# Softmax attention with 48 and 49 contraction rows and 17 value columns in place of 63, 64 and 32

## What is computed

```python
x = x + _layernorm(_L0_attn_ref(_layernorm(x, axis=-1), L0_attn_w_attn, L0_attn_w_proj), axis=-1)
x = x + _layernorm(_L0_ffn_ref(_layernorm(x, axis=-1), ...), axis=-1)
x = x + _layernorm(_L1_attn_ref(_layernorm(x, axis=-1), ...), axis=-1)   # linear attention
x = x + _layernorm(_L1_ffn_ref(_layernorm(x, axis=-1), ...), axis=-1)
```

```python
attn = jnp.einsum('bhqd,bhkd->bhqk', q, k) * scale
attn = jnp.where(causal[None, None], attn, -jnp.inf)
sm = jax.nn.softmax(attn, axis=-1)
out = jnp.einsum('bhqk,bhkd->bhqd', sm, v)
```

## Time and profile before

| | |
|---|---|
| median of 3 runs | 4012.15 us (4011.11 to 4018.99) |
| profiled execution, its time | 4022.0 us |
| its span (first to last instruction) | 4020.2 us |
| PE busy | 3221.1 us, 80% |
| PEld busy | 2353.4 us, 59% |
| DVE busy | 2413.5 us, 60% |
| ACT busy | 1504.5 us, 37% |
| mean granted TensorE clock | 0.884 of full speed |

### The profile page before, as it was taken

One profiled execution on the slowest core, in us unless ns is written; L12 is line 12 of the kernel. 1 busy time (PEld: TensorE's weight loads), 2 busy tenths in 40 slices (PEclk: granted clock), 3 DMA queues, 4 the chain that ended last, 5 costly groups with the idle time before them and its releaser, 6 DMA issues. The chain is left out here.

```text
span 4020.2 us, 61755 instructions
## 1 busy us (share of the span) xinstructions
PE 3221.1 (80%) x20641; PEld 2353.4 (59%) x20641; DVE 2413.5 (60%) x6322; ACT 1504.5 (37%) x2158; POOL 809.5 (20%) x873
## 2 busy tenths in 40 slices
PE   6859888888887666596655768998666499999998
PEld 5633333333333565495434556776565488888887
DVE  5557777777774677661227865544677444444444
ACT  2316666666666333242005650000233233333333
POOL 0011111121112222245765651000122000000000
PEclk9868999999999788698658988999777699999999
DMA  7893455444551565644658996665444513233332
GB/s 191 240 157 51 75 85 79 72 71 75 84 77 36 170 216 176 236 141 118 139 116 262 345 309 190 217 200 160 142 156 147 171 45 84 83 83 83 83 83 52
DMA packets 448954, 553.07 MB, mean 138 GB/s; under 512 B 96592, under 2 KB 301424, under 8 KB 447600
## 3 DMA queue, kind: packets, MB, share of 16 engines
q1 hardware_dynamic: 436992, 527.15, 49.3%
q0 software_dynamic: 10240, 14.16, 2.1%
q10 hardware_dynamic: 1648, 10.81, 0.8%
HBM read 312.85 MB, written 238.61 MB: 137 GB/s over the span
## 5 line engine op out<-in xcount | busy, mean ns | idle before, releaser
L545 ACT ACTIVATE att_pr<-att_e_ps 128x1024 f32<-128x1024 f32 (+2 forms) x640 | 596.2, 940 | 326.8 <-PE att_e_ps L597 323.2
L573 PE MATMUL att_m_ps<-att_ks,att_qs 63*128 63x512 f32 (+3 forms) x1536 | 493.9, 446 | 125.1 <-DVE att_mx L510 54.1
L573 PEld LDWEIGHTS att_m_ps<-att_ks,att_qs 63*128 63x128 f32 x1536 | 233.3, 191 | 520.6 <-DVE att_mx L507 185.8
L507 DVE CUSTOM_DVE_ANT_0 att_kept<-att_m_ps,att_causal 128x128 f32<-128x128 f32 (+3 forms) x1024 | 448.3, 487 | 76.1 <-PE att_m_ps L573 52.2
L510 DVE TENSOR_REDUCE att_mx<-att_m_ps 128x1 f32<-128x512 f32 x512 | 329.6, 686 | 158.4 <-PE att_m_ps L573 154.8
L614 PE MATMUL att_o_ps<-att_pr,att_vs 128*32 128x512 f32 (+3 forms) x3072 | 338.2, 513 | 28.3 <-issue 28.1
L486 POOL TENSOR_SCALAR_AFFINE_SELECT att_pr<-att_pr 128x256 f32<-128x256 f32 (+1 forms) x384 | 186.5, 486 | 850.7 <-PEq L588 814.2
L597 PE MATMUL att_e_ps<-att_qs,att_ks 64*128 64x512 f32 (+3 forms) x1536 | 321.1, 376 | 1.8 <-ACT att_pr L545 1.3
L2138 DVE TENSOR_TENSOR ffn_hid<-ffn_gate,ffn_u_ps 128x512 f32<-128x512 f32 x192 | 132.1, 688 | 251.4 <-PE ffn_u_ps L720 208.1
L2186 ACT ACTIVATE ffn_hh<-ffn_hid 128x512 fp32r<-128x512 f32 x192 | 121.6, 633 | 422.8 <-DVE ffn_hid L2142 320.7
L2148 DVE TENSOR_TENSOR ffn_hl<-ffn_hid,ffn_hh 128x512 fp32r<-128x512 f32 x192 | 133.0, 693 | 141.9 <-ACT ffn_hh L2186 141.9
(11 more groups left out here) (287 smaller groups left out, 8075.3 us busy)
## 6 DMA issues: line engine op xcount, KB each, us to landing
prj_o<-attended SPq DMA_DIRECT2D x32, 1024.0 KB
ffn_wt<-weights SPq DMA_DIRECT2D x16, 2048.0 KB
att_qs<-q_high SPq DMA_DIRECT2D x128, 128.0 KB, 5.5
att_ks<-k_high SPq DMA_DIRECT2D x128, 128.0 KB, 7.0
attended<-att_ot SPq DMA_DIRECT2D x64, 256.0 KB, 2.0
prj_x<-x SPq DMA_DIRECT2D x32, 512.0 KB, 5.9
x_high<-prj_xh SPq DMA_DIRECT2D x32, 512.0 KB, 2.8
x_low<-prj_xl SPq DMA_DIRECT2D x32, 512.0 KB, 3.8
```

The lines of the kernel that those rows point to most:

```text
L507: e.tensor_tensor_reduce(kept[:, n % MBUF, 0:w], m_ps[:, n % MBUF, 0:w], causal[:, BLK - w:], 1.0, -3e38, ALU.add, ALU.max, mx[:, h, at, q ...
L545: e.activation(out, src, ACT.Exp).then_inc(exp_done, 1)
L573: e.matmul(m_ps[:, (2 * i + n) % MBUF, 0:w], qs[rows, j, p, q * P:(q + 1) * P], ks[rows, j, p, h * BLK:h * BLK + w], start=True, stop=True ...
```

## The change

Three numbers and what hangs on them. The maximum pass contracts over the 48 rows that hold data, where it took 63; the row for the maximum is row 48 of each half instead of row 63, so the scores contract over 49 rows, where they took 64; and a product with the values loads 17 columns for each head, where it loaded 32. The zero columns behind the last head, and the memset that wrote them, go. Nothing is added, and no instruction changes its place: on every engine the rest stands in the same order with the same semaphores, except that PE's first wait counts two constants instead of three. Partitions 17 to 31 of each head's strip of `o_ps` are no longer written by PE; they keep the zeros of the memset of `o_ps` (L497), and are copied and stored as before. The two halves (64 rows) and the four strips (32 partitions) on which the matmuls are placed in the array remain.

```diff
-    HALF, MAXROW, VSTEP = P // 2, P // 2 - 1, GH * VW + 32 - VW
+    HALF, MAXROW, VSTEP = P // 2, 3 * HD, GH * VW
...
-                e.memset(vs[:, :, :, GH * VW:].rearrange("p j k c -> p (j k) c"), 0.0).then_inc(consts_pe, 1)
                 e.memset(o_ps[:], 0.0).then_inc(consts_pe, 1)
...
                     for hd in range(GH):
-                        i = e.matmul(o_ps[32 * hd:32 * hd + 32, BLK - w:BLK], vs[:, j, k, hd * VW:hd * VW + 32],
+                        i = e.matmul(o_ps[32 * hd:32 * hd + VW, BLK - w:BLK], vs[:, j, k, hd * VW:(hd + 1) * VW],
                                      pr[:, u % NPR, hd // 2, hd % 2, 0:w], start=k == 0, stop=k == 4 * h + 3)
...
-                e.wait_ge(consts_pe, 3)
+                e.wait_ge(consts_pe, 2)
```

## The result

The changed kernel takes 4210.95 us (median, 4206.82 to 4214.52), the kernel before 4015.57 in the same comparison: ratio 1.0486, 95% interval 1.0467 to 1.0504, +195 us. Forecast was 4400 in a range of 4150 to 4570. The direction and the cause were right, and 4211 lies in the range, near its lower end; the likeliest value had twice the growth that came.

A forecast was written before the change was run, and what follows sets the result against it. PE was taken to bound the attention once slow: 31 groups x 13 us at 1.2 GHz = 403, less 23 already paid, plus 9 for the last group, +389; forecast 4400 us, range 4150 to 4570.

The forecast's parts named there:

- PE is thus the bound as soon as it is slow.: Softmax attention: PE is fullest, busy 78.84 of 90 us; 6.8 us at 1.2 GHz cost a group 2.61 us.
- Busy time alone doesn't tell when the clock is full.: First maximum passes: PE busy 29.53 of 40 us at clock 0.50; wide work, products above all, stands where full clock holds.
- the rival of no change: Attention clock stays, as the chip counts halves and strips or busy time: 4012 less at most 5 us; chance 0.12.
- No row shows whether the chip counts the rows and columns that an instruction names or the halves and strips on which it is placed.: Attention matmuls: left open; costs 0 if nothing is counted differently, otherwise the clock is lost.
- the weight 17/32 = 0.53: Products with the values: with 17 columns for 32 they fill 0.53 of the array they filled before.
- Stretch (c): Attention, 450.6 to 454.39 us: no products run, clock then falls with PE 82% busy; taken to show little to spare.
- Once at 1.2 GHz nothing in the loop is as wide as what brought the clock back. I take it that the whole phase then runs at 1.2 GHz.: Whole attention phase at 1.2 GHz: +389 us, forecast 4400; chance 0.72.
- The rival of partial low clock: Attention clock falls but products bring it back repeatedly; about half the phase at 1.2 GHz: +195, 4207 us; chance 0.13.
- The price at 1.2 GHz: Attention group at 1.2 GHz: products +7.7, scores +3.4, maxima +4.9 us, less PE's idle waits; taken as +13 us.
- the upper end of +17.9: Attention group at 1.2 GHz costs at most +17.9 us, from a whole stretch taking 1.58 times as long; gives 4553 us.
- The rival "faster": Idle time before product matmuls, 28.3 us, shrinks with shorter weight loads: 3984 us at the most; chance 0.03.
- Cost of the memset and of the DMAs at nothing: Before the loop: removed memset gains 0 to 0.5 us; the row maximum takes the same two DMAs.

The follow-up runs named there:

- e3: Kernel before with only the maximum pass cut from 63 to 48 rows (scores 64 rows, products 32 columns): 4117.80 us, ratio 1.0252.
- e7: Kernel before with 56 rows in the maximum pass and 57 in the scores, 32 value columns: 4109.85 us, ratio 1.0222.
- e11: Kernel before with only the scores cut to 49 rows (maximum pass 63 rows, 32 value columns): 4104.11 us, ratio 1.0203.
- e2: Kernel before with only the products cut from 32 to 17 columns (63 and 64 rows kept, memset kept): 3999.15 us, ratio 0.9954.
- e9: e2 with the transposition of the maxima issued twice in each group, once for nothing: 4010.11 us, ratio 0.9977 of the kernel before.
- e4: Kernel before, shapes kept, with the product matmuls of the unit of step 16 issued ahead of the maximum matmuls: 4009.42 us, ratio 0.9982.
- e8: Changed kernel plus 8 extra matmuls a group (128 rows, 128 columns, 512 elements), results overwritten: 4182.33 us, ratio 1.0407 of the kernel before.
- e10: e5 plus two extra matmuls a group of 128 rows and 512 elements, ahead of score steps 3 and 9: 4000.43 us, ratio 0.9952 of the kernel before.
- e12: Changed kernel with the transposition of the maxima issued twice in each group: 4239.83 us, ratio 1.0560 of the kernel before.
- e5: Kernel before with 17 value columns, 63 and 64 rows, and the products of the unit of step 16 issued first: 4012.90 us, ratio 0.9983.
- e1: Kernel before with only the rows cut (maximum pass 48, scores 49), products keeping 32 columns: 4250.26 us, ratio 1.0571.

## Why the prediction was right in direction and cause, and wrong in size

- **"PE is thus the bound as soon as it is slow."** Right. All 190.5 us lie between the merges; the busy time of DVE, ACT and POOL stayed.
- **"Busy time alone doesn't tell when the clock is full."** Right, and e3 shows it best: groups busy for 27.16 us as before, then 23 us at half clock, with no instruction more or less. The Trainium skill ("TensorE: Matmul & The Clock Gate", Part 1: The HAM clock gate) has the gate watch how busy PE is; by that the rival of no change should have come, at 4012. The trace goes against it in this form: with groups at full clock that are busy for one and the same 88%, maximum passes of 48, 56 and 63 rows give clocks of 0.87 (e3), 0.86 (e7, scores at 57 too) and 0.98.
- **"No row shows whether the chip counts the rows and columns that an instruction names or the halves and strips on which it is placed."** It was open and is settled for rows: named rows count, those that hold zeros too (e3, e7, e11), at an unchanged half of 64. For columns from 32 to 17 no effect was found (e2, e9); the weight 17/32 = 0.53 that I gave the products was wrong.
- **Stretch (c), the fall behind 3.8 us without products,** was read too strongly. The transposition, 128 rows at 453.80, runs in it as well, and the same stretch stands in each group, most of which keep the clock. Before, a group earlier:

```profile
418.74 1.06 PE L614 MATMUL att_o_ps<-att_pr,att_vs 128*32 128x512 f32 x8
...
423.51 1.07 PE L614 MATMUL att_o_ps<-att_pr,att_vs 128*32 128x512 f32 x8
```

No fall follows there, and with the products moved ahead of it (e4) falls got more, not fewer.
- **The step that failed:** "Once at 1.2 GHz nothing in the loop is as wide as what brought the clock back. I take it that the whole phase then runs at 1.2 GHz." It rested on the columns. The products have 128 rows whatever their columns, and two of them bring the clock back at the same place as before. So the low share of the loop is 20.5 of 37.6 us, 55%, not all. That the rows of the products are what brings it back fits e8 and e10, and no run takes rows from them to show it.
- **The rival of partial low clock** gave 4207 and came, at 4211, with a chance of only 0.13. Its argument for, that products take a growing share of time at the low clock, fits the timeline; the argument against it was the same error about columns. That it came within 4 us is luck: its +195 was no sum of its own but half of the full price, and one matmul of 0.13 us more in a group moves the changed kernel by 29 us (e12).
- **The price at 1.2 GHz** was probably a little low. By an estimate from e2's full group of 30.73 us and the changed kernel's stretches: less 17.1 it leaves 13.6 us of work for 20.5 low ones, so a low us does the work of 0.67; a group wholly low would take some 46 us, +15.5, between my +13 and the upper end of +17.9. No run was low throughout. The product's 1.86 us was 1.84.
- **The rival "faster"** didn't come: the idle time before the product matmuls is 28.2 us in the changed kernel and 28.7 in e2, as before with 28.3. What does come of the shorter loads is the 13 ns a unit of its argument against, 5 us in all, seen in e2. I had put it at nothing since the clock would swallow it, and in the changed kernel it can't be told from the rest.
- **Cost of the memset and of the DMAs at nothing:** the start of the loop, 283.2 against 285.2 us, moved by 2 us. In the experiments that keep the memset it lies anywhere from 282.5 us (e5) to 287.1 (e10), so 2 us is within the scatter and nothing is seen of either.

## What to carry to other kernels

A matmul that contracts over fewer rows can cost the loop its clock, though at a given clock it takes the same time itself. Before trimming zero rows from a contraction in a loop whose granted clock lies near 1.0 with TensorE idle now and then, look for stretches that already fall, and try the trimmed version against the padded; here the padding of 15 rows was worth 233 us of 4017 (e1). Columns can be trimmed rather: the weight load gets shorter, and at 17 no loss of clock was found. And small gains in such a loop (under 0.5%) have to be tried at a slightly different pace as well, since falls come and go with it.

## What was not expected of the hardware

- Rows of a matmul that are 1.0 times 0.0 help to hold the clock: leaving them out of the maximum pass costs 2.5% (e3).
- The relation looks graded: 63/64 rows 4017, 56/57 rows 4110, 48/49 rows 4250 us, all on the same halves of the array. How each size would move with the length of a group was tried for 48/49 and 63/64 rows alone, each with 17 columns (29 us in e12, 9 in e9).
- The turns of the clock lock to the loop. In the changed kernel, from 359 to 1431 us, every low stretch is 20.5 us and every full one 17.1, group after group. One more matmul of 0.13 us in a group breaks this and costs 29 us; in e2 it costs 9 to 11.
- Extra work can pay: 256 matmuls more, with 140.9 us of busy time, made the changed kernel 29 us faster (e8).
- The fastest kernel here is e2, 63 and 64 rows with 17 columns: 3999.15 us, 0.9954 of before (0.9938 to 0.9971); e10 is level with it.
